# Queries read from PSUM, dummy matmuls in TensorE's gaps, and a later restore in a two-stage attention kernel

## What is computed

```python
x = x + _L0_conv_ref(_gn(x), ...)   # dilated 3x3 attention, 4 dilations, gated
x = x + _L1_conv_ref(_gn(x), ...)   # channel attention in 4 heads, projection

# stage 1, for dilation i of (1, 2, 4, 8): 32 channels, 2 heads of 16
qkv  = einsum('bchw,oc->bohw', x, w_qkv)
attn = einsum('bhdn,bhdkn->bhnk', q, unfold3x3(k, dil)) * 16 ** -0.5
out  = einsum('bhnk,bhdkn->bnhd', softmax(attn), unfold3x3(v, dil))
gate = softmax(mean_hw(x) @ w_gate.T + b_gate)       # one number per dilation
```

## Time and profile before

| | us |
|---|---|
| median of 3 runs | 88.88 |
| lowest and highest of the runs | 87.90, 91.84 |
| time of the profiled execution | 89.51 |
| its span, first to last instruction | 87.60 |
| VectorE busy | 72.9 (83%) |
| TensorE matmuls busy | 68.2 (78%) |
| GpSimd busy | 43.8 (50%) |
| ScalarE busy | 31.3 (36%) |

### The profile page before, as it was taken

One profiled execution on the slowest core, in us unless ns is written; L12 is line 12 of the kernel. 1 busy time (PEld: TensorE's weight loads), 2 busy tenths in 40 slices (PEclk: granted clock), 3 DMA queues, 4 the chain that ended last, 5 costly groups with the idle time before them and its releaser, 6 DMA issues.

```text
span 87.6 us, 2173 instructions
## 1 busy us (share of the span) xinstructions
PE 68.2 (78%) x860; PEld 50.7 (58%) x860; DVE 72.9 (83%) x191; ACT 31.3 (36%) x99; POOL 43.8 (50%) x82
## 2 busy tenths in 40 slices
PE   0199998998967297290998989974999986999950
PEld 0199785575524164260887857664877654866830
DVE  1178499999999999999989778999894999866970
ACT  4486699161670000000011004210856355286320
POOL 7004486059100099992999989799970001400000
PEclk9999999999999999999855699997557999999999
DMA  1993012000000000000000000000000000002235
GB/s 9 330 356 86 0 27 71 0 0 7 0 0 4 4 7 0 0 0 0 4 7 0 0 0 0 0 0 7 0 0 0 0 0 0 11 33 87 64 129 174
DMA packets 3019, 3.11 MB, mean 35 GB/s; under 512 B 320, under 2 KB 2752, under 8 KB 3008
## 3 DMA queue, kind: packets, MB, share of 16 engines
q1 hardware_dynamic: 2576, 2.69, 9.6%
q10 hardware_dynamic: 432, 0.26, 1.2%
HBM read 1.91 MB, written 1.05 MB: 34 GB/s over the span
## 4 chain that ended last, share of the span: by engine, by line
DVE 45%; PE 26%; POOL 12%; issue 7%; DMA 4%; ACT 1%; POOLq 1%; ACTq 0%
PE ps L753 24%; DVE qk L561 22%; DVE pv L602 10%; POOL acc L333 6%; POOL pv L333 5%; DMA xt<-x_dram 4%; DVE x L621 3%; PE ps L881 2%; DVE ssum L578 1%; DVE gsq L508 1%; DVE x L647 1%; DVE acc L614 1%; POOLq L99 1%; POOL rstd L298 1%; DVE smax L568 1%
## 5 line engine op out<-in xcount | busy, mean ns | idle before, releaser
L753 PE MATMUL ps<-prob,sel 64*128 64x192 f32 (+6 forms) x192 | 19.3, 342 | 8.8 <-DVE pv L602 8.2
L753 PEld LDWEIGHTS ps<-prob,sel 64*128 64x128 f32 x192 | 15.7, 215 | 12.9 <-DVE pv L602 11.4
L561 DVE TENSOR_TENSOR qk<-q,k 128x128 f32<-128x128 f32 (+7 forms) x36 | 21.3, 658 | 0.1
L602 DVE TENSOR_TENSOR pv<-ps,v 128x128 f32<-128x128 f32 (+7 forms) x32 | 16.9, 568 | 3.0 <-PE ps L753 1.7
L753 PE MATMUL ps<-xn,wp 128*32 128x256 f32 (+1 forms) x208 | 18.0, 392 | 0.1
L333 POOL TENSOR_TENSOR pv<-pv 128x240 f32<-128x240 f32 (+3 forms) x24 | 15.6, 660 | 1.7 <-DVE pv L602 1.5
L753 PEld LDWEIGHTS ps<-xn,wp 128*32 128x32 f32 (+1 forms) x208 | 11.1, 121 | 4.7 <-DVE xn L655 0.6
L298 POOL TENSOR_TENSOR rstd<-gvar,mhalf 128x2 f32<-128x2 f32 (+1 forms) x6 | 4.9, 824 | 16.5 <-DVE gvar L509 16.4
L333 POOL TENSOR_TENSOR acc<-acc,pv 128x256 f32<-128x256 f32 (+4 forms) x20 | 12.9, 647 | 0.5
L753 PE MATMUL ps<-xt 128*128 128x128 f32 x28 | 7.1, 437 | 4.0 <-DMA xt<-x_dram 4.0
L753 PE MATMUL ps<-qk,cs 128*32 128x192 f32 (+6 forms) x176 | 8.3, 317 | 1.1 <-ACT v L378 0.7
(11 more groups left out here) (74 smaller groups left out, 91.6 us busy)
## 6 DMA issues: line engine op xcount, KB each, us to landing
xt<-x_dram SPq DMA_DIRECT2D x4, 256.0 KB, 3.8
out_dram<-x SPq DMA_DIRECT2D x8, 128.0 KB, 1.9
wp<-wpack_dram SPq DMA_DIRECT2D x1, 325.0 KB, 5.5
sel<-selc_dram SPq DMA_DIRECT2D x4, 64.0 KB, 4.1
cs<-consts_dram ACTq DMA_DIRECT2D x1, 130.0 KB, 3.1
cs<-consts_dram ACTq DMA_DIRECT2D x2, 64.0 KB, 2.6
```

The source lines that it names most:

```text
L561: last = nc.vector.tensor_tensor(o, a, b, ALU.mult)
L602: last = nc.vector.tensor_tensor(o, a, b, ALU.mult)
L753: return nc.tensor.matmul(o, w, m, start=start, stop=stop)
```

## The change

Three things change.

1. The query tiles of units 2 and 3 of the second half are no longer projected into a rotating bank and copied (22 tiles are left). `project_query(s)` writes them into the two halves of PSUM bank 4 once the first half's scores there have been read (`shift_ready`), between tiles 17 and 18, and `multiply_qk` reads them there. `restore(0)`, which writes bank 4, waits for all products.
2. `keep_clock` calls are placed in TensorE's order from `sum_scores(1, 0)` on: 19 matmuls in eight places instead of 5 in one place. They write bank 5, later bank 7 and bank 0.
3. On TensorE `restore(0)` comes after `spread(1, 1, 0)` instead of after `spread(1, 0, 1)`, and `group_stats(0)` and `restore(1)` move one spread later with it. VectorE's order follows: `first_residual(0)`, `second_variance(0)` and `first_residual(1)` come two and one multiplies later.

```diff
+        Q_IN_PSUM = [(0, s, PHASES - 1) for s in range(2, ND)]
+        def q_columns(s):
+            return 512 * SC[0] + N * (s % 2)
...
-            tiles += [(kind, s, ph) for s in range(ND) for kind in (0, 1)] + [(2, s, ph) for s in range(ND)]
+            tiles += [(kind, s, ph) for s in range(ND) for kind in (0, 1) if (kind, s, ph) not in Q_IN_PSUM]
+            tiles += [(2, s, ph) for s in range(ND)]
...
-            for n in range(18, 24):
+            for n in range(18, len(tiles)):
                 copy_tile(n)
...
+                in_psum = (0, s, ph) in Q_IN_PSUM
+                if in_psum and ci == 0:
+                    dve.wait_ge(q_ready, len(Q_IN_PSUM))
...
-                    a = view(q, (s * PHASES + ph) * N + r0 * W + c0, [[dr * W, n], [W, rows], [1, c1 - c0]])
+                    a = view(ps if in_psum else q, (q_columns(s) if in_psum else (s * PHASES + ph) * N) + r0 * W + c0,
+                             [[dr * W, n], [W, rows], [1, c1 - c0]])
...
-            for i in range(2):
+            for i in range(3):
                 multiply_pv(1, 0, i)
+            multiply_pv(1, 1, 0)
             first_residual(0)
-            multiply_pv(1, 0, 2)
-            multiply_pv(1, 1, 0)
+            multiply_pv(1, 1, 1)
             second_variance(0)
             first_residual(1)
-            for i in range(1, 3):
-                multiply_pv(1, 1, i)
+            multiply_pv(1, 1, 2)
             second_variance(1)
...
-            def keep_clock(n, shifted=0):
-
-                if shifted:
-                    pe.wait_ge(shift_ready, shifted)
+            def keep_clock(n, bank=IDLE_BANK):
+
                 for _ in range(n):
-                    mm(ps[:, IDLE_BANK, 0:P], xt[:, 0, 0:P], xt[:, 0, 0:P])
+                    mm(ps[:, bank, 0:P], xt[:, 0, 0:P], xt[:, 0, 0:P])
...
+            def project_query(s):
+
+                pe.wait_ge(shift_ready, 1)
+                for j in range(SLOTS):
+                    last = mm(view(ps, q_columns(s), [[1, N]], 32 * j, 32), wp[:, W_QKV + CD * s:W_QKV + CD * s + CD],
+                              xn[:, PHASES * j + PHASES - 1, :])
+                last.then_inc(q_ready, 1)
...
                 if ph == 0:
                     pe.wait_ge(shift_ready, g + 1)
+                    pe.wait_ge(qk_ready, ND * PHASES)
...
-            for n in range(15, 24):
+            for n in range(15, 18):
+                project(n)
+            for i in range(2, ND):
+                project_query(i)
+            for n in range(18, len(tiles)):
                 project(n)
             sum_scores(1, 0)
-            for i in range(3):
+            for i in range(2):
                 spread(0, 0, i)
+            keep_clock(3)
+            spread(0, 0, 2)
             for i in range(2):
                 spread(0, 1, i)
             sum_scores(1, 1)
+            keep_clock(1)
             spread(0, 1, 2)
             spread(0, 2, 0)
             sum_scores(1, 2)
+            keep_clock(1)
             for i in range(1, 3):
                 spread(0, 2, i)
             sum_scores(1, 3)
+            for i in range(2):
+                spread(0, 3, i)
+            keep_clock(2)
+            spread(0, 3, 2)
+            keep_clock(6)
             for i in range(3):
-                spread(0, 3, i)
-            keep_clock(2, 1)
-            keep_clock(3, 1)
-            for i in range(2):
                 spread(1, 0, i)
+            spread(1, 1, 0)
             restore(0)
-            spread(1, 0, 2)
-            spread(1, 1, 0)
+            spread(1, 1, 1)
             group_stats(0)
             restore(1)
-            for i in range(1, 3):
-                spread(1, 1, i)
+            spread(1, 1, 2)
             group_stats(1)
-            for i in range(3):
+            for i in range(2):
                 spread(1, 2, i)
+            keep_clock(2, BANK[1] + 1)
+            spread(1, 2, 2)
+            keep_clock(1, BANK[1] + 1)
             spread(1, 3, 0)
...
             attention(1)
+            pe.wait_ge(pv_ready, 12 * PHASES)
+            keep_clock(3, BANK[2])
             restore(2)
```

More of the change, by code:

```diff
@@ L194, in build @@
         proj_copied = sem("proj_copied")
+        q_ready = sem("q_ready")
         qk_ready = sem("qk_ready")
```

## The result

The changed kernel takes 84.3 us (median of 4 runs, 84.17 to 86.43); the kernel before beside it takes 89.29 us (4 runs, 87.9 to 91.84). The ratio is 0.951, with a 95% interval of 0.946 to 0.956. The profiled execution took 84.39 us with a span of 82.6; before it was 89.51 and 87.6. The forecast was 84.0 us, from a sum that gave a span of 82.3.

What follows compares the result with a forecast made beforehand. VectorE was taken as the bound, slowed by GpSimd's additions and waits at half clock. Terms 3.6 + 0.8 - 0.4 + 1.3 = 5.3 us took the span from 87.60 to 82.3; forecast 84.0 us, range 82.4 to 86.6.

Steps and rivals of the forecast that it cites:

- Queries from PSUM: Second half's units 2 and 3: PSUM queries escape GpSimd's slowing, ten products fall from 6.77 to 3.1 us, gain 3.6.
- From the products to the second half: Up to the second half's first multiply: full clock shortens VectorE's wait from 1.1 to 0.5 us; gain 0.8.
- Dummies: 19 dummies in TensorE's waits for VectorE, 0.31 us each at full clock, all hidden there.
- Restore two spreads later: restore(0) meets GpSimd's end at 48.9 without waiting; price 0.4 us, while the old place would lose about 1 us.
- of which VectorE has 0.9 us of work as cover: At restore(0) in the old order: TensorE waits 1.8 us, VectorE's work covers 0.9, a loss of about 1 us.
- The second slow stretch: Second-stage projections and last spreads at full clock: VectorE's 1.18 us wait and a 0.2 us one go; gain 1.3.
- what bounds there next is VectorE's own work: After the waits before the second half's last spreads go, VectorE's work sets the pace, limiting the gain to 1.3 us.
- The rivals: Clock falls again 20, GpSimd bounds 10, products stay slow 6, TensorE bounds 3, more than the sum 10, in 100.
- The rival in which the clock falls once more: One fall costs 0.5 us in the first stretch or 1.2 to 1.8 in the second: 84.7 to 86.0 us; 20 in 100.
- The rival in which the products stay slow: The second SBUF operand is not what slows q*k; only the clock's part is left: 86.8 to 87.6 us; 6 in 100.
- at most 2.2 us: The clock's part of the gain, left if the products stay slow.

Runs made afterwards that it cites:

- e5_last_three: The changed kernel with only five dummies before the second half's first spread and three before restore(2); ratio to the kernel before 0.953.
- e2_no_psum: The changed kernel with all 24 tiles projected and copied, so queries are read from SBUF; ratio to the kernel before 1.001.
- e1_psum_only: The kernel before with only the queries in PSUM added, old dummies and old orders kept; 87.38 us, ratio to the kernel before 0.984.
- e4_old_restore: The changed kernel with restore(0), group statistics and residuals in their old places on TensorE and VectorE; 87.92 us, ratio to the kernel before 0.991.
- e3_old_dummies: The changed kernel with only the five old dummies before the second half's first spread; 85.59 us, ratio to the kernel before 0.966.
- v1_early_products: The changed kernel with unit 3's last multiplies after two additions of unit 2, their spreads earlier, one dummy before restore(2); 84.57 us, ratio to before 0.944.
- e6_no_dummies: The changed kernel without any dummy from the score sums on; 86.70 us, ratio to the kernel before 0.973.
- e10_vector_old: The changed kernel with the old order of residuals and variance on VectorE alone; 85.94 us, ratio to the kernel before 0.966.
- e8_twelve: The changed kernel with twelve dummies instead of six before the second half's first spread; ratio to the kernel before 0.961.

## Why the prediction came out

The time, the direction and the mechanism were right: 84.3 us for 84.0. The sum was 0.4 us too large, two terms having come out larger and two smaller; the first multiply came 0.15 us later and the tail was 0.2 us shorter, which the sum had at nothing. That the errors partly cancel is chance, but all of them are small. The four terms, from the starts of VectorE's rows of before and after:

| term | forecast | measured |
|---|---|---|
| products, first multiply to the row at 40.67 / 37.07 | 3.6 | 11.00 - 7.25 = 3.75 |
| from there to the second half's first multiply | 0.8 | 10.25 - 9.39 = 0.86 |
| from there to unit 2's first multiply, 59.53 / 55.66 | -0.4 | 8.61 - 9.20 = -0.59 |
| from there to restore(2) | 1.3 | 10.76 - 9.85 = 0.91 |
| sum | 5.3 | 4.93 |

- **Queries from PSUM** was right in size and cause. The ten products took 3.05 us for the 3.1 that were worked out. The Trainium skill, VectorE: DVE Perf Modes, the section on the TRN2 errata, would have them dearer by 62 cycles each; the trace does not agree: 0.419 us from PSUM against 0.412 from SBUF. The query groups were free as foretold: the score sums started at 26.81, 1.0 us later, and VectorE's first multiply did not wait.
- **From the products to the second half** was right: probabilities at 44.49 + 0.89 = 45.38 (45.5), dummies over at 44.65 (44.8), first multiply at 46.46 (46.5). The wait was 0.68 instead of 0.5.
- **Dummies** cost 0.245 to 0.27 us each in the long groups, 0.31 as forecast in a group of three, up to 0.49 when alone, and were hidden. What the prediction did not see is that most of them were not what kept the clock up in the middle stretch of a good execution: the old five alone gave the same middle stretch.
- **Restore two spreads later** was right in the changed kernel: GpSimd done with the first half at 48.80 + 0.46 = 49.26 (48.9). Wrong was the price of the old place, 2.4 us and not about 1. The step that failed is "of which VectorE has 0.9 us of work as cover": VectorE's own order has the residual ahead of that work, so it had none, and the clock fell behind the wait.
- **The second slow stretch** was a term too large by 0.4 us. The wait of 1.18 us went and the projections took 2.17 us, less than the 2.45 of the working. But the step "what bounds there next is VectorE's own work" took that work at its old length. Four additions of 128x192 grew from 0.382 to 0.567 us, 0.74 us in all, beside more of GpSimd's additions than before. No run takes GpSimd out of this place, but its additions slowing work on two SBUF tensors is what the prediction itself had read from the products.
- **The rivals.** None of them came. GpSimd did come onto the chain of waits: its additions stand there from 31.66 to 49.27 us, and `restore(0)` reached TensorE just as it ended. So there it is as long a path as VectorE's, and not above it. The rival in which the clock falls once more is what `e5_last_three` shows. It put 0.5 us on a fall in the first stretch, by the dummies; there it was 36.95 - 35.69 = 1.3 us, because the spreads ahead of and behind the dummies were slow too. The rival in which the products stay slow has its run in `e2_no_psum`: it gave that case 86.8 to 87.6 us, and the run was no faster than before (a gain of up to 1.2% is inside its interval), so what was left for the clock alone, "at most 2.2 us", was put too high.

The parts do not add up one by one. By the middle stretch the queries in PSUM are worth 3.6 us with the later restore and 2.45 without it; the later restore is worth 2.4 with them; the dummies and the later restore together 1.3 without them, which the timed runs do not confirm. The added dummies gave nothing in the old order (38.17 us in `e1_psum_only` with the old five, 38.11 in `e4_old_restore` with all 19) and 0.97 us in the new one (35.70 + 18.05 in `e3_old_dummies` against 35.69 + 17.09); against none at all they gave 1.6. Neither the added dummies nor the later restore was run alone on the kernel before. A sum of single worths would be wrong by more than 1 us either way; the forecast worked out each term with the others in place.

## What to carry to other kernels

When VectorE multiplies two SBUF tensors while GpSimd adds in SBUF, look for the same shape at an idle moment of GpSimd: if it is twice as fast there, as here (0.412 and 0.865 us), put one operand in PSUM, and then look at what reaches the next shared wait earlier. An instruction that waits for another engine has to be moved in the queues of all engines that take part in the exchange, and its cover is what stands ahead of it in each queue, not what stands behind. Dummy matmuls belong in TensorE's longest waits ahead of work on the path (here the clock fell behind waits of 1.33 us and more, not every time); count what hides them, and measure several executions, since the same kernel keeps the clock in some and loses it in others.

## What the runs showed of the hardware

**The start is slow for a different time in each execution.** TensorE's first matmul records, in order of time, in the changed kernel and in `v1_early_products`, whose code is the same up to there:
```profile
6.30 2.15 PE L763 MATMUL ps<-xt 128*128 128x128 f32 x10
...
9.01 5.52 PE L763 MATMUL ps<-xn,wp 128*32 128x256 f32 x88 [0.37 <-DVE xn L545]
```
```profile
6.08 2.48 PE L764 MATMUL ps<-xt 128*128 128x128 f32 x10
...
9.67 7.07 PE L764 MATMUL ps<-xn,wp 128*32 128x256 f32 x88
```
Ten records in 2.48 us is the price of the half clock in the earlier trace rows (2.50 us at 47.47), yet the profile has the granted clock full here. In the changed kernel the quicker pace is there before the projections begin; in the other one a projection record takes 0.63 us until about 13 us, and 0.38 afterwards. The 88 records took 5.52 to 5.81 us in five profiles (before and after among them) and 6.84 to 7.07 in the other eight, the slow execution of the next paragraph aside. The copy of the first key, for which the first product waits, starts at 10.6 to 10.8 us in the five and at 11.4 to 12.2 in the others, and this is carried to the end. It accounts for most of the 2 us by which executions differ; what decides when the pace changes, no run here shows.

**One execution at several times the matmul time.** When the changed kernel was run again, its profiled execution took 207.62 us, with TensorE busy 97% of the span at a full granted clock and its projections at 1.10 us a record instead of 0.38; the three others took 84.24 to 84.4. 

> The changed kernel itself, beside the runs below on one chip: 84.2 to 84.6 us.

The three agree with the first runs of this kernel; for the one there is no explanation here.

**Waits and the clock.** In these profiles every fall of the clock in the middle stretch and at `restore(2)` came behind a wait of TensorE of 1.33 us or more. Such waits were often followed by a fall (1.33 in `e5_last_three`, 1.44 in `e1_psum_only`, 1.49 in `e3_old_dummies` and `e6_no_dummies`, 1.87 in `e2_no_psum`, 2.34 in `e4_old_restore`) and often not: the same wait of 1.33 us in `e1_psum_only`, `e3_old_dummies` and `e6_no_dummies`, 1.37 in `e10_vector_old`, 1.61 in before, and 2.29 in the earlier trace rows, behind which 16 records took 1.58 us, the time of the full clock. The changed kernel, `e8_twelve` and `v1_early_products`, all with the full clock, have none above 0.8 us there. I had looked only at waits of 2.3 us as a danger.

**Small instructions last longer too.** A two-element instruction of VectorE on SBUF takes 0.16 us behind 68 us, where GpSimd has no additions. Beside them it takes between 0.16 and 0.70 us (0.34 at 52.28 and 0.70 at 55.03 above). That the additions are the cause is argued from the products; no run takes them away here.
